# A graph network on one core: a semaphore for each sum and each block step, an address without an AND, longer loops

## What is computed

```python
h = relu(layernorm(x)); x = x + L0(h)   # messages sqrt(softmax in * softmax out) * h[src], summed by dst
h = relu(layernorm(x)); x = x + L1(h)   # two attention passes:
    # e = beta * cos(h[src], h[dst]); p = softmax of e over the edges of dst; h = relu(sum of p * h[src])
h = relu(layernorm(x)); x = x + L2(h)   # sum over edges of h[src] @ weight[type of 16]
h = relu(layernorm(x)); x = x + L3(h)   # the same with 32 types, mean over edges, + h @ self_weight + bias
```

## Time and profile before

| | |
|---|---|
| median of 3 runs | 16613.94 us (16609.46 to 16620.77) |
| the profiled execution, its own time | 16705.54 us |
| its span | 16703.7 us |
| busy: PE, PEld (weight loads), DVE | 7120.6, 6075.7, 6471.3 us |
| busy: ACT, POOL | 2680.9, 9403.8 us |
| granted clock of TensorE, mean | 0.502, its lower level of 1.2 GHz |

### The profile page before, as it was taken

How to read it: one execution, slowest core, us unless ns; L and a number is a source line. 1 busy time by engine, 2 the same in 40 slices (tenths; PEclk the granted TensorE clock), 3 DMA queues, 4 the chain that set the end, 5 groups by cost and what they waited for, 6 DMA issues and landing times. The chain is left out here.

```text
span 16703.7 us, 167845 instructions
## 1 busy us (share of the span) xinstructions
PE 7120.6 (43%) x35085; PEld 6075.7 (36%) x35140; DVE 6471.3 (39%) x18639; ACT 2680.9 (16%) x7299; POOL 9403.8 (56%) x9933
## 2 busy tenths in 40 slices
PE   4311112222222566666656666665333334333333
PEld 1100001222222555555555555554323233223323
DVE  3322224333333455555545555554222223222222
ACT  0000000000000333333333333333000000000000
POOL 5476763655555555555545555554656656566666
PEclk5555555555555555555555555555555555555555
DMA  1000001111111111111121111112111112111111
GB/s 29 3 5 5 5 4 44 22 21 21 21 21 19 37 36 39 36 36 39 36 38 42 46 42 42 43 42 37 39 38 40 40 38 44 31 23 23 23 23 22
DMA packets 429667, 499.79 MB, mean 30 GB/s; under 512 B 235856, under 2 KB 245584, under 8 KB 417584
## 3 DMA queue, kind: packets, MB, share of 16 engines
q0 software_dynamic: 317504, 279.59, 10.7%
q1 hardware_dynamic: 97730, 214.09, 3.8%
q10 hardware_dynamic: 14316, 4.81, 0.1%
HBM read 397.49 MB, written 94.54 MB: 29 GB/s over the span
## 5 line engine op out<-in xcount | busy, mean ns | idle before, releaser
L680 POOL DMA_INDIRECT Z<-table,idx x4986 | 4703.3, 943 | 4326.8 <-issue 1700.3
L1575 PE MATMUL ps<-Z 128*128 128x65 f32 x9972 | 2313.9, 419 | 4972.2 <-DVE pay_d L1367 2504.1
L1575 PEld LDWEIGHTS ps<-Z 128*128 128x128 f32 x9972 | 2189.5, 329 | 5209.0 <-issue 5065.3
L1367 DVE SCALAR_TENSOR_TENSOR pay_d<-pay_d,ps 128x65 f32 x4986 | 1110.2, 223 | 4000.0 <-issue 2976.3
L680 POOL DMA_INDIRECT Z<-table_a,idx x1662 | 1567.8, 943 | 1090.1 <-issue 549.0
L656 POOL DMA_INDIRECT bins_dst<-slot_d x1612 | 1561.5, 969 | 959.4 <-issue 495.7
L680 POOL DMA_INDIRECT Z<-table_b,idx x1662 | 1567.9, 943 | 894.1 <-issue 514.6
L1562 PE MATMUL ps<-Z 128*128 128x65 f32 x6648 | 1532.9, 418 | 275.1 <-DVE pay_d L1214 213.1
L1562 PEld LDWEIGHTS ps<-Z 128*128 128x128 f32 x6648 | 1468.5, 331 | 361.1 <-DVE Z L1202 240.0
L1529 PE MATMUL ps<-pay_d,Z 128*128 x6648 | 1532.9, 421 | 33.2 <-ACT Z L738 31.1
L1529 PEld LDWEIGHTS ps<-pay_d,Z 128*128 128x128 f32 x6648 | 1485.5, 333 | 32.4 <-issue 32.1
(11 more groups left out here) (245 smaller groups left out, 7975.3 us busy)
## 6 DMA issues: line engine op xcount, KB each, us to landing
pay_d<-locals_ SPq DMA_DIRECT2D x92, 1152.0 KB
Z<-table,idx POOLq DMA_INDIRECT x4986
table_b<-pay_d SPq DMA_DIRECT2D x192, 256.0 KB
Z<-table_a,idx POOLq DMA_INDIRECT x1662
Z<-table_b,idx POOLq DMA_INDIRECT x1662
bins_dst<-slot_d POOLq DMA_INDIRECT x1612
table_a<-kept SPq DMA_DIRECT2D x94, 256.0 KB
slot_d<-pay_d SPq DMA_DIRECT2D x62, 91.0 KB
```

Of the source, the lines that this page charges most:

```text
L680: nc.gpsimd.indirect_dma_start(rows[:, at.slot, j, 0:width], None, ps_.table, bass.IndirectOffsetOnAxis(ap=idx[:, at.slot, j:j + 1], axis= ...
L1367: v.scalar_tensor_tensor(out=of_block, in0=of_block, scalar=1.0, in1=p_pair[:, at.two, j * ROW:(j + 1) * ROW], op0=ALU.mult, op1=ALU.add). ...
L1575: last = mm(p_pair[:, at.two, j * ROW:(j + 1) * ROW], hot_d[:, at.three, j, :], given, start=True, stop=True)
```

## The change

1. The five semaphore-sharing sums get a semaphore each: `item_added[j]` is raised once a group by sum j, and the next sum waits for `done(e + at.g)` on it, the value that the group's first sum waits for on `summed`. `added` is the last of the six, in all passes. `sum_added`, `sum_part`, `part_added` and `hot_f_direct` fall away (one-hots raise `hot_f_made` in all passes), and `own` with them: all waits count with `every`, and the semaphores that only attention passes use start NG higher.
2. Each step k of a block gets a semaphore `blk_step(k)`, 15 in all, raised once a block in the passes that have such a step. Its value is `rank.n` plus a constant.
3. The lower place of a word is unpacked as `two - (two >> 12) * 4096`.
4. The loops have 44 rounds for 42, and the blocks 44, 45 and 46 behind them are finished in two portions in successive groups (0, then 1 to 5), a block every two groups.

```diff
         self.loops = (self.groups - RING) // RING - 1
-        self.loops -= 2 + self.loops % 2
+        self.loops -= self.loops % 2
...
-            for k, later in enumerate((0, 1, 1, 2, 2, 2)):
+            for k, later in enumerate((0, 1, 1, 1, 1, 1)):
                 self.rest.setdefault(at + later, []).append((r, k))
-            at += 3
+            at += 2
...
-        blk_step, blk_root = sem("blk_step"), sem("blk_root")
+        blk_steps = [sem(f"blk_step{k}") for k in range(1, 16)]
+        blk_root = sem("blk_root")
...
-        msg_made, summed, added, part_added = sem("msg_made"), sem("summed"), sem("added"), sem("part_added")
+        msg_made, summed = sem("msg_made"), sem("summed")
+        item_added = [sem(f"item_added{j}") for j in range(ITEMS)]
+        added = item_added[ITEMS - 1]
...
             two = at.known[j // 2]
-            one = (two & 4095, two >> 12)[j % 2]
+            one = (two - (two >> 12) * 4096, two >> 12)[j % 2]
...
+        def blk_step(k):
+            return blk_steps[k - 1]
+
         def step_of(p, rank, k):
-            return rank.n * OPS[p] + (sum(OPS[:p]) * NB + k)
+            return rank.n + (sum(OPS[q] >= k for q in range(p)) * NB + 1)
...
             def store_rows(p, r):
...
-                sp.wait_ge(blk_step, step_of(p, rank, OPS[p]))
+                sp.wait_ge(blk_step(OPS[p]), step_of(p, rank, OPS[p]))
...
                 def narrow_hots(at):
-                    act.wait_ge(pen_made, done(own + at.g))
-                    act.wait_ge(edge_max, done(own + at.g - RING))
+                    act.wait_ge(pen_made, done(e + at.g))
+                    act.wait_ge(edge_max, done(e + at.g - RING))
...
                 def sum_of(j):
                     def one_sum(at):
                         if j == 0:
                             dve.wait_ge(summed, done(e + at.g))
-                            dve.wait_ge(keep_made, done(own + at.g))
-                            dve.wait_ge(added, done(own + at.g - 1))
+                            dve.wait_ge(keep_made, done(e + at.g))
+                            dve.wait_ge(added, done(e + at.g - 1))
                         else:
-                            dve.wait_ge(part_added, (own + at.g) * (ITEMS - 1) + j)
+                            dve.wait_ge(item_added[j - 1], done(e + at.g))
...
                 def then(rank, k, ins):
-                    ins.then_inc(blk_step, 1)
-                    dve.wait_ge(blk_step, step_of(p, rank, k))
+                    ins.then_inc(blk_step(k), 1)
+                    dve.wait_ge(blk_step(k), step_of(p, rank, k))
...
                 def direct_sum(j):
                     def one_sum(at):
                         if j == 0:
                             dve.wait_ge(summed, done(e + at.g))
-                            dve.wait_ge(sum_added, done(own + at.g - 1))
+                            dve.wait_ge(added, done(e + at.g - 1))
                         else:
-                            dve.wait_ge(sum_part, (own + at.g) * (ITEMS - 1) + j)
+                            dve.wait_ge(item_added[j - 1], done(e + at.g))
                         of_block = acc[:, bass.ds(place_at(at, j), ROW)]
                         v.scalar_tensor_tensor(out=of_block, in0=of_block, scalar=1.0, in1=p_pair[:, at.two, j * ROW:(j + 1) * ROW],
-                                               op0=ALU.mult, op1=ALU.add).then_inc(sum_added if j == ITEMS - 1 else sum_part, 1)
+                                               op0=ALU.mult, op1=ALU.add).then_inc(item_added[j], 1)
...
                 def sums_per_node(at):
-                    pe.wait_ge(sum_added, done(own + at.g - 2))
-                    pe.wait_ge(hot_f_direct, done(own + at.g))
+                    pe.wait_ge(added, done(e + at.g - 2))
+                    pe.wait_ge(hot_f_made, done(e + at.g))
```

More of the change, by code:

```diff
@@ L379, in gnn_program, with __init__ @@
         class Pass:
-            def __init__(self, kind, every, gather, own, column=0, table=None):
+            def __init__(self, kind, every, gather, column=0, table=None):
                 self.p = every
@@ L716, in work @@
             def work(ps_):
-                e, own = ps_.every, ps_.own
+                e = ps_.every
                 def rows_wanted(at):
@@ L724, in penalty @@
                 def penalty(at):
-                    act.wait_ge(local_loaded[at.part], 16 * (own // NG * LOADS[at.part] + at.turn + 1))
-                    act.wait_ge(spread, done(own + at.g - RING))
+                    act.wait_ge(local_loaded[at.part], 16 * ((ps_.p - 1) * LOADS[at.part] + at.turn + 1))
+                    act.wait_ge(spread, done(e + at.g - RING))
                     nc.scalar.activation(pen_t[:, at.slot, :], local_row[:, at.part, at.slot * ITEMS * P:(at.slot + 1) * ITEMS * P],
@@ L806, in work @@
                 if ps_.softmax:
-                    act.wait_ge(units_made, own // NG + 1)
+                    act.wait_ge(units_made, p)
                     act.wait_ge(local_stored, LOCAL_STORES)
@@ L848, in _ @@
         def _(dve):
-            for s in (factor_kept, hot_f_made, hot_f_direct, multiplied, dotted, scored, group_max, max_made, risen,
-                      shift_made, msg_made, added, sum_added):
+            for s in [factor_kept, hot_f_made, msg_made] + item_added:
                 dve.sem_inc(s, CREDIT)
+            for s in (multiplied, dotted, scored, group_max, max_made, risen, shift_made):
+                dve.sem_inc(s, CREDIT + NG)
             steps = [0]
@@ L1141, in one_hots @@
                         dve.wait_ge(summed, done(e + at.g - 3))
-                        v.tensor_tensor(hot_d[:, at.three, :, :], every, nodes, ALU.is_equal).then_inc(hot_f_direct, 1)
+                        v.tensor_tensor(hot_d[:, at.three, :, :], every, nodes, ALU.is_equal).then_inc(hot_f_made, 1)
                     if ps_.kind == EDGE:
@@ L1177, in rises @@
                     o = at.slot * ITEMS
-                    dve.wait_ge(max_made, done(own + at.g))
+                    dve.wait_ge(max_made, done(e + at.g))
                     if at.slot == 0:
@@ L1215, in one_sum @@
                                                in1=p_items[:, j * ROW:(j + 1) * ROW], op0=ALU.mult,
-                                               op1=ALU.add).then_inc(added if j == ITEMS - 1 else part_added, 1)
+                                               op1=ALU.add).then_inc(item_added[j], 1)
                     return one_sum
@@ L1230, in whole @@
                     rank.place = known.with_bounds(min_val=0, max_val=(pl.banks - 1) * 512 + (PER_BANK - 1) * ROW)
-                    if ps_.softmax:
-                        dve.wait_ge(added, done(own + rank.last))
-                    else:
-                        dve.wait_ge(sum_added, done(own + rank.last))
+                    dve.wait_ge(added, done(e + rank.last))
                     return acc[:, bass.ds(rank.place, D)], acc[:, bass.ds(rank.place + D, 1)]
@@ L1428, in _ @@
         def _(pe):
-            for s in (dst_rows, spread, edge_max, summed):
-                pe.sem_inc(s, CREDIT)
+            pe.sem_inc(summed, CREDIT)
+            for s in (dst_rows, spread, edge_max):
+                pe.sem_inc(s, CREDIT + NG)
             for s in (part_made, blk_turned):
@@ L1520, in work @@
             def work(ps_):
-                e, own = ps_.every, ps_.own
+                e = ps_.every
                 def rows_of_destinations(at):
-                    pe.wait_ge(hot_32_made, done(own + at.g))
-                    pe.wait_ge(multiplied, done(own + at.g - 2))
+                    pe.wait_ge(hot_32_made, done(e + at.g))
+                    pe.wait_ge(multiplied, done(e + at.g - 2))
                     for j in range(ITEMS):
@@ L1556, in sums_per_item @@
                 def sums_per_item(at):
-                    pe.wait_ge(added, done(own + at.g - 1))
-                    pe.wait_ge(hot_f_made, done(own + at.g))
+                    pe.wait_ge(added, done(e + at.g - 1))
+                    pe.wait_ge(hot_f_made, done(e + at.g))
                     pe.wait_ge(msg_made, done(ps_.gather + at.g))
-                    pe.wait_ge(mass_made, done(own + at.g))
+                    pe.wait_ge(mass_made, done(e + at.g))
                     for j in range(ITEMS):
```

84 lines of the change are left out of this document (43 added, 41 removed).

## The result

The kernel after takes **16398.8 us** (median of 4 runs, 16392.1 to 16463.7) where the kernel before takes 16611.7 (4 runs, 16548.8 to 16620.8): ratio 0.9889, 95% interval 0.9854 to 0.9924, 1.1% faster. The prediction said 2.5%. The two profiled executions, 16403.95 and 16705.5 us, differ by 302 us, but that of before was 94 us above its median, so they overstate the gain.

What follows compares the result with a forecast made beforehand. No engine is full; POOL pauses for DVE's sums, slow at 0.7 us an instruction while POOL issues. -282 (direct sums) -143 (attention) +15 (loops) = -410 us from 16705.5: 16295 profiled, 16204 in the runs; range 15850 to 16590.

Steps and rivals of the forecast that it cites:

- Rival E: Whole change: it doesn't remove what it says, instructions fall by less than a tenth; 16614 us within 0.2%; chance 0.09.
- the 0.15 us: Direct sums: an even place loses one 45 ns operation from the chain, taking DVE's quick group from 4.3 to 4.15 us.
- In one cycle of POOL's (run, pause) let G groups pass: Edge and relational passes: equation of DVE's quick and slow time per POOL cycle; gains 87, 113 and 82, together 282 us.
- while POOL issues without a pause, every DVE instruction, register arithmetic too, costs 0.7 us: DVE in all passes: the number of instructions, not their work, is the price in slow stretches, 0.706 us each.
- 143 us: Both attention passes: fewer step operations in each round's block, half counted, (2.4 + 1.0) us x 42 rounds; ends nothing and 290.
- the 101 us of the second pass: Second attention pass: seven of nine slow step operations go, 4.9 us a round, half counted as 2.4 over 42 rounds.
- worth nothing there: Attention passes: 5 wait and 3 AND operations less a group gain nothing, since DVE waits for PE; otherwise 200 us.
- Loops: 44 rounds, three blocks behind them: extra waits between DVE and ACT cost +15 us, from 0 to 30.
- Base: Sum made against the profiled 16705.5 us, its difference carried in microseconds to the runs' median of 16613.9.
- C: DVE's slow speed isn't one of instructions but a port or memory stall; gain 120 us, 16490 us; chance 0.14.
- D: Attention passes: quicker DVE lets POOL run on, one more 6.3 us stall each round, 570 us; 16780 us, slower; chance 0.10.
- B: Feedback weaker than thought: POOL hardly pauses, half of 1449 us plus the attention passes' 143; about 15750 us; chance 0.17.

Runs made afterwards that it cites:

- the probe: Kernel before and kernel after, each with a semaphore for every direct-sum matmul and ACT copying a column on seeing it: 16633.6 and 16335.8 us.
- after_b: The kernel after, unchanged, run again on chip A: median 16409.8 us, ratio 0.9893 to the kernel before; edge pass 2649 us.

## Why the prediction was half right

**Counts: right.** The register operations of L1365, the ANDs of L1367 and most of the steps went. Rival E falls. One detail was wrong: in quick stretches the merged operation of an even place takes 201 to 217 ns, where the pair took 45 and 53, and that of an odd place 46 to 53 for 92 to 107, so six quick sums last 2.35 us (15214.49 to 0.58 behind 15216.26) for 2.31 before (15504.95 to 0.22 behind 15507.04), and nothing of the 0.15 us was gained.

**The step that failed** is the one that begins "In one cycle of POOL's (run, pause) let G groups pass". It wrote the equation for DVE's instructions alone and made 282 us of it, where the pair of profiles shows 172. PE's products come late in the same stretches, some 4.2 us an item, by an estimate from the probe's gaps 25 us a group for DVE's 20 in the last pass; the change doesn't touch that. The prediction had a sign of it in the earlier trace rows, where DVE stood 6.32 us for products whose rows lay ten microseconds back, and kept it for the attention passes. So 82 us of the last pass became 27, with 1123 us of waiting for PE where 1090 of slow operations had been. In the first relational pass, where DVE had 32 instructions a group, 113 became 127 in this pair; how much of that is luck is open, since the same pass took 2644 us in the probe of the kernel before, 57 more than in the profile that was read. In the edge pass 87 became 18. That pass also moves by itself: the probe on ACT alone took it to 2557 us, 92 below after_b, for a cause that stays open.

**Under it, a premise was too strong**: "while POOL issues without a pause, every DVE instruction, register arithmetic too, costs 0.7 us". The price as measured was right on this chip, but it is no property of instructions beside gathers. On chips B and C it is absent beside gathers without any pause. And on chip A it spares an engine that has just waited: at 13994.02, 21 us into a run of POOL's, DVE's sums are quick. That, and the word of ten products let go within 1.15 us after a pause of POOL's, reads like a store that empties at a slow rate and holds back the engine when full; it is argued, not shown. The Trainium skill has a place that could be it: "NOTIFIC — the notification-queue block", § 7.1, says that the block that writes the engines' records holds an engine back rather than lose one inside. No run here shows that block.

**Attention passes: the sum nearly fitted, the reason did not.** Forecast 143 us, 120 in the pair of profiles. But the 101 us of the second pass were put down to the steps of a block, and putting these back gave 18 us less, not more. The probe of the kernel before had this pass at 3012 us for the 3083 of the profile that was read, so about 70 of the 111 us lie between executions of one kernel. The five operations that were "worth nothing there" brought 23 us in the second pass and -5 in the first, which one execution of each can't tell from nothing.

**Loops: not refuted**, 21 us for 15, within the spread of the runs. **Base:** I carried a difference of profiles over in microseconds. The profiled execution's excess was largely in one pass, and the gain by medians is 182 to 213 us.

**The rivals.** C gave nearly the measured size, 120 us for 182 to 213, with a wrong reason: register operations do slow down on chip A. The rule that the prediction cites beside it from the Trainium skill ("SBUF — State Buffer", § SBUF: two separate sides; contention at a shared port alone) does not explain them. D's mechanism came, in the other passes: long waits at the sums for PE's late products, which took back the gain and no more. B's half is what it never came near: even with both engines' work halved the last pass keeps 270 us above the floor.

**What stays open:** single parts put back make 65 of the 182 us on chip A. The rest is the AND's, or comes only of the parts together. Open are also why chip A slows DVE's instructions and the delivery of PE's products, and whether PE's matmuls are slow themselves. The equation for two engines names the right parties but not the sizes: it gave 545 us where 299 came.

## What to carry to other kernels

If a trace shows instructions of every kind stretched to one duration, ask first whether it is the kernel's or the chip's: a second chip gave the old kernel 23% and the parts of the change nothing. Where one engine is seen to be slow, write the balance for every engine that works in the same stretch, and place a stamp on an idle engine where the profile only models the end. Count which row a product belongs to before its lateness is read, and look whether late products come one by one or in a burst. Sum against the median, with a second profile before a pass's length is made a term.

## What was not expected of the hardware

The same program took 16460 to 16591 us on chip A and 12801 to 12823 on chips B and C, at a granted TensorE clock of 0.50 (1.2 GHz) on all of them. Nearly all of the difference lies where POOL issues its DMAs: in the passes, 13751 us for 10421 together in the two profiles, and in the stretch ahead of them, 2710 us for 2176. PE's matmul rows stood at 0.43 us an item while the products were seen some 4.2 us apart, or ten within 1.15 us behind a pause of POOL's. And ACT, which has few instructions there, never ran the fused operation ahead of its row copies slower than 93 ns while DVE's went to 1411 (ns min/median/max, first profile of the kernel after):

```profile
L728 ACTq FUSED_REGOPS  x1320: 64/69/93, 2762.6 to 16315.6; - x189
```
